# First expert layer of batches 4 to 7 computed per chosen expert instead of for all three experts

## The reference, cut to what matters

```python
h = _layernorm(x)
router_input = concatenate([h, modality_ratio], axis=-1)
gate_scores = softmax(router_input @ gate_w + gate_b)
top_val, top_idx = top_k(gate_scores, 2)
top_val = top_val / (sum(top_val) + 1e-8)
pre = einsum('bsd,edf->ebsf', h, w1) + b1
act = stack([tanh(pre[0]), gelu(pre[1]), silu(pre[2])])
expert_out = einsum('ebsf,efd->ebsd', act, w2) + b2
for i in range(2):
    moe_out += top_val[..., i:i+1] * expert_out[top_idx[:, 0, i], batch]
x = x + tanh(g_ffn[0]) * moe_out
```

## Time and profile before

| | us |
|---|---|
| median of 3 runs | 724.17 (723.84 to 725.5) |
| the profiled execution | 722.57 |
| its span | 720.8 |
| PE busy | 698.6 (97%) |
| DVE busy | 544.8 (76%) |
| ACT busy | 357.4 (50%) |
| POOL busy | 419.2 (58%) |
| mean granted TensorE clock | 0.997 |

### The profile page before, as it was taken

How to read it: one execution, slowest core, us unless ns; L and a number is a source line. 1 busy time by engine, 2 the same in 40 slices (tenths; PEclk the granted TensorE clock), 3 DMA queues, 4 the chain that set the end, 5 groups by cost and what they waited for, 6 DMA issues and landing times.

```text
span 720.8 us, 11347 instructions
## 1 busy us (share of the span) xinstructions
PE 698.6 (97%) x3478; PEld 585.7 (81%) x3478; DVE 544.8 (76%) x908; ACT 357.4 (50%) x955; POOL 419.2 (58%) x356
## 2 busy tenths in 40 slices
PE   7799998999999999999999999999999889999998
PEld 5688887888888888888888888888888667788886
DVE  6478686788788887888878788787887984478832
ACT  7424633554545545455454545545455675772130
POOL 4698764766667566665666657666676542473020
PEclk9999999999999999999999999999999999999999
DMA  8887566323222141131322213112222410230101
GB/s 292 290 245 283 207 207 200 89 59 88 60 76 73 30 119 58 58 88 61 85 59 82 64 36 110 58 58 88 69 78 59 120 59 28 74 117 1 58 1 59
DMA packets 66110, 71.09 MB, mean 99 GB/s; under 512 B 8592, under 2 KB 42384, under 8 KB 66064
## 3 DMA queue, kind: packets, MB, share of 16 engines
q1 hardware_dynamic: 65680, 69.51, 30.8%
q0 software_dynamic: 384, 1.05, 0.5%
HBM read 51.66 MB, written 18.87 MB: 98 GB/s over the span
## 4 chain that ended last, share of the span: by engine, by line
PE 89%; DVE 3%; ACT 2%; DMA 2%; POOL 2%; issue 1%; SPq 1%; ACTq 0%; POOLq 0%; DVEq 0%
PE q L272 39%; PE y L262 28%; PE o L621 5%; PE s L573 5%; PE pt L479 4%; PE s L575 2%; PE s L262 2%; PE o L262 2%; PE pt L262 2%; ACT prob L869 1%; DMA prob<-rope_rows,posi 1%; POOL rot L1044 1%; DMA rows<-ctx_t 1%; DMA wraw<-in_L_xattn_Wq 1%; DVE split L1153 1%
## 5 line engine op out<-in xcount | busy, mean ns | idle before, releaser
L272 PE MATMUL q<-xT_hi,big 128*128 128x512 f32 x704 | 237.1, 402 | 0.4 <-issue 0.4
L262 PE MATMUL y<-big,split 128*128 128x512 f32 (+1 forms) x784 | 191.6, 390 | 2.9 <-DVE split L1153 2.9
L262 PEld LDWEIGHTS y<-big,split 128*128 128x128 f32 x784 | 146.7, 188 | 34.2 <-DVE split L1153 3.9
L272 PEld LDWEIGHTS q<-xT_hi,big 128*128 128x128 f32 x704 | 132.9, 189 | 27.6 <-issue 0.6
L272 PE MATMUL q<-xT_lo,big 128*128 128x512 f32 x352 | 137.5, 391 | 0.0
L1100 POOL TENSOR_TENSOR roped<-rot 128x512 f32<-128x512 f32 x59 | 76.2, 1292 | 104.3 <-DVE rot L1177 104.3
L869 ACT ACTIVATE prob<-scores,nmax 128x128 f32<-128x128 f32 x256 | 99.9, 392 | 22.1 <-DVE nmax L1278 22.1
L857 ACT ACTIVATE big<-roped 128x512 fp32r<-128x512 f32 x64 | 40.5, 634 | 140.6 <-POOL roped L1100 136.1
L1116 POOL TENSOR_TENSOR prob<-prob,prec 128x512 f32<-128x512 f32 x64 | 66.6, 1040 | 50.4 <-DVE prec L1292 50.4
L1104 POOL TENSOR_TENSOR big<-roped,big 128x512 fp32r<-128x512 f32 x64 | 82.7, 1293 | 13.2 <-ACT big L857 13.2
L1092 POOL TENSOR_TENSOR big<-wraw,big 128x512 fp32r<-128x512 f32 x64 | 83.0, 1298 | 0.0
(11 more groups left out here) (187 smaller groups left out, 1160.2 us busy)
## 6 DMA issues: line engine op xcount, KB each, us to landing
wraw<-in_L_xattn_Wq SPq DMA_DIRECT2D x32, 256.0 KB
wraw<-in_L_xattn_Wo SPq DMA_DIRECT2D x32, 256.0 KB
kv<-k_scratch SPq DMA_DIRECT2D x64, 128.0 KB, 2.5
kv<-v_scratch SPq DMA_DIRECT2D x64, 128.0 KB, 2.8
wraw<-in_L_ffn_w SPq DMA_DIRECT2D x28, 256.0 KB
v_scratch<-split SPq DMA_DIRECT2D x12, 512.0 KB, 4.1
k_scratch<-split SPq DMA_DIRECT2D x10, 512.0 KB, 3.2
k_scratch<-kv SPq DMA_DIRECT2D x6, 512.0 KB, 3.6
```

What stands on the lines that cost most here:

```text
L262: mm = pe.matmul(bank_[:, :], stationary(s, c), moving(m, c), start=(c == 0 and n == 0), stop=(c == EC - 1 and n == 2))
L272: mm = pe.matmul(bank_[:, :].rearrange("p (b t) -> p b t", b=BH), weights[s][:, c, h * P:(h + 1) * P], source[m][:, half * BH:(half + 1) * ...
```

## The change

Batches 0 to 3 are left as they are. For batches 4 to 7 the 12 tiles of all experts are replaced by 8 tiles, one for each batch and slot ("pair" j = 0 to 7; 0 to 3 are slot 1 and 4 to 7 are slot 0 of batches 4 to 7).

- `pair_first(j)` on PE: xT of the batch is stationary, and w1 of the chosen expert moves, its block number read into a register from `pick_row`. Tokens lie on the partitions, so that b1 can't be a per-partition bias.
- `pair_add(j)` on DVE: the bank plus the b1 row of each of the two experts that the slot may hold, into two SBUF tiles. The b1 rows are loaded by three broadcast DMAs into `rows`.
- `pair_act(j)` on ACT: both functions, in place. For slot 1 they are silu and gelu, in an order that alternates with j; for slot 0 tanh and gelu.
- `pair_select(j)` on DVE: predicated copy of the second over the first.
- `pair_transpose(j)` on PE: four transposes into `tbank`; `pair_hi_(j)` on ACT and `pair_lo_(j)` on DVE split it; two buffers in `split`.
- The second layer goes by `second_tile(u)`. The four first-layer tiles that stood between tile 11 and the second layer are no more there.
- The second w1[0] goes to block 5 of `big` (where the hi and lo parts of slot 0 of batches 0 to 3 are), and its hi parts wait for second-layer tile 3 (`f2` of 4) instead of first-layer tile 15. SP waits for the last pick of batches 0 to 3 before the b1 rows and these four chunks.
- DVE: bias(0), then bias(u+1) and add_slot(u) for u = 0 to 6, then the pairs. Two small operations are added ahead of `picks_ok`.

```diff
+EXPERT_BLOCK = (0, 1, 2, 0, 4, 3, 5)
+FIRST = [(e, f) for e in range(NX) for f in range(EC)]
+PAIRS = [(slot, BH + k) for hf, slot, k in SECOND if hf == 1]
+SLOT_EXPERTS = ((0, 1), (2, 1))
...
+        b1row = [rows[:, e, :] for e in range(NX)]
+        def pair_at(j):
+            return split[:, (2, 0)[j % 2], :, :]
+        def both(j):
+            return kept[2 * (j % 2):2 * (j % 2) + 2]
+        def turn_of(j):
+            return (1, 0) if PAIRS[j][0] == 1 and j % 2 == 1 else (0, 1)
...
             for n in range(W_A + KVH * W_PER + LAG_Y, W_END):
+                if n == W_C + 6 * EC:
+                    sp.wait_ge(f_pick, EC)
+                    for e in range(NX):
+                        sp.dma_start(b1row[e], bcast(b1[e], E)).then_inc(b1_in, 16)
                 w_load(n, expert_chunk(n)).then_inc(w_in[n % NW], 16)
...
+            def second_tile(u):
+                hf, slot, k = SECOND[u]
+                j = u - B
+                if u == 0:
                     pe.wait_ge(w_lo, W_C + 6 * EC)
                     pe.wait_ge(picks_ok, 1)
+                if hf == 1:
+                    pe.wait_ge(pair_lo, j + 1)
+                elif k == 0:
+                    pe.wait_ge((keep_lo, pick_lo)[slot], EC)
+                e = pe.value_load(pick_row[0:1, slot * B + hf * BH + k:slot * B + hf * BH + k + 1],
+                                  min_val=0, max_val=NX - 1)
+                if u < 2:
+                    pe.wait_ge(y_acc, UNITS - 1 + u)
+                elif u >= 4:
+                    pe.wait_ge(f_acc, u - 3)
...
+            def pair_first(j):
+                slot, b = PAIRS[j]
+                at = 2 * B + slot * BH + b - BH
+                n = pe.value_load(pick_row[0:1, at:at + 1], min_val=0, max_val=5)
+                if j == 0:
+                    pe.wait_ge(h_lo, B)
+                if j == BH:
+                    pe.wait_ge(w_lo, W_END)
+                if j < 2:
+                    pe.wait_ge(f_act, len(FIRST) - 1 + j)
+                else:
+                    pe.wait_ge(f_z, 2 * (j - 1))
+                project(pe, qbank[j % 2], lambda a, c: xT[a][:, b, c, :],
+                        lambda a, c: big[:, bass.ds(n, 1), a, c * 512:(c + 1) * 512].rearrange(
+                            "p n k -> p (n k)")).then_inc(f1, 1)
+
+            def pair_transpose(j):
+                pe.wait_ge(f_sel, j + 1)
+                if j >= 1:
+                    pe.wait_ge(pair_lo, j)
+                transpose4(tbank, lambda c: both(j)[0][:, c * P:(c + 1) * P], f_t)
...
-            for l in range(NX * EC, (NX + 1) * EC):
-                first_layer(l)
-            second_layer(0, 0)
-            second_layer(0, 1)
-            for l in range((NX + 1) * EC, 2 * NX * EC):
-                first_layer(l)
-            second_layer(1, 0)
-            second_layer(1, 1)
+            for u in range(B - 1):
+                second_tile(u)
+            for j in range(B):
+                pair_first(j)
+                if j >= 1:
+                    pair_transpose(j - 1)
+                if j != 1:
+                    second_tile(B + j - 2 if j >= 2 else B - 1)
+            pair_transpose(B - 1)
+            second_tile(2 * B - 2)
+            second_tile(2 * B - 1)
...
                 if n == W_C + 6 * EC:
-                    act.wait_ge(f1, 4 * EC)
+                    act.wait_ge(f2, BH)
...
+            def pair_act(j):
+                for n, which in enumerate(turn_of(j)):
+                    e = SLOT_EXPERTS[PAIRS[j][0]][which]
+                    act.wait_ge(f_z, 2 * j + n + 1)
+                    act.activation(both(j)[which], both(j)[which], (ACT.Tanh, ACT.Gelu, ACT.Silu)[e]).then_inc(f_fn, 1)
+
+            def pair_hi_(j):
+                act.wait_ge(f_t, j + 1)
+                if j >= 1:
+                    act.wait_ge(f2, B + j - 1)
+                else:
+                    act.wait_ge(y_done, UNITS)
+                act.activation(pair_at(j)[:, 0, :], tbank[:, :], ACT.Copy).then_inc(pair_hi, 1)
...
             for f in range(EC):
                 w_expert_hi(n + 13 + f)
+            pair_act(0)
+            for j in range(1, B):
+                pair_hi_(j - 1)
+                pair_act(j)
+            pair_hi_(B - 1)
...
+            ts(pick_row[:, 2 * B:2 * B + BH], out_of[:, 0, BH:B], -4.0, 5.0, ALU.mult, ALU.add)
+            ts(pick_row[:, 2 * B + BH:2 * B + 2 * BH], in_it[:, 1, BH:B], -1.0, 1.0, ALU.mult, ALU.add)
...
+            def pair_add(j):
+                for n, which in enumerate(turn_of(j)):
+                    if n == 0:
+                        dve.wait_ge(f1, len(FIRST) + j + 1)
+                        if j == 0:
+                            dve.wait_ge(b1_in, 16 * NX)
+                            dve.wait_ge(keep_lo, EC)
+                        if j >= 2:
+                            dve.wait_ge(f_t, j - 1)
+                    dve.tensor_tensor(both(j)[which], qbank[j % 2][:, :], b1row[SLOT_EXPERTS[PAIRS[j][0]][which]], ALU.add
+                                      ).then_inc(f_z, 1)
+
+            def pair_select(j):
+                slot, b = PAIRS[j]
+                dve.wait_ge(f_fn, 2 * j + 2)
+                dve.copy_predicated(both(j)[0], masks[:, slot, b:b + 1].to_broadcast([P, 512]), both(j)[1]
+                                    ).then_inc(f_sel, 1)
+
+            def pair_lo_(j):
+                dve.wait_ge(pair_hi, j + 1)
+                subtract_hi(pair_at(j)[:, 1, :], tbank[:, :], pair_at(j)[:, 0, :], pair_lo)
...
-            for u in range(B):
-                bias(u)
+            bias(0)
+            for u in range(B - 1):
+                bias(u + 1)
                 add_slot(u)
...
+            for j in range(B):
+                pair_add(j)
+                if j >= 1:
+                    pair_lo_(j - 1)
+                pair_select(j)
+                if j != 1:
+                    add_slot(B + j - 2 if j >= 2 else B - 1)
+            pair_lo_(B - 1)
+            add_slot(2 * B - 2)
+            add_slot(2 * B - 1)
```

More of the change, by code:

```diff
@@ L192, in build @@
         f2, f_acc, f_bias = sem("f2"), sem("f_acc"), sem("f_bias")
-        b2_in = sem("b2_in")
+        b1_in, b2_in = sem("b1_in"), sem("b2_in")
+        f_z, f_fn, f_sel, f_t = sem("f_z"), sem("f_fn"), sem("f_sel"), sem("f_t")
+        pair_hi, pair_lo = sem("pair_hi"), sem("pair_lo")
         out_done = sem("out_done")
@@ L202, in build @@
         w1_at = [[block_of(n, s) for s in range(2)] for n in (0, 1, 0)]
-        w2_at = [[block_of(n, s) for s in range(2)] for n in (2, 3, 4)]
         w2_all = big[:, 2:2 + NX, :, :]
@@ L369, in expert_target @@
         def expert_target(n):
-            (layer, e), k = expert_matrix(n)
-            return (w1_at, w2_at)[layer][e], k
+            at = EXPERT_BLOCK[(n - W_C) // EC]
+            return [block_of(at, s) for s in range(2)], (n - W_C) % EC
         block = stack.enter_context(nc.Block())
@@ L666, in first_layer @@
                     pe.wait_ge(f_act, l - 1)
-                project_tile(pe, qbank[l % 2], w1_at[e], f, xT, hf).then_inc(f1, 1)
+                project_tile(pe, qbank[l % 2], w1_at[e], f, xT, 0).then_inc(f1, 1)
             groups(pe, unit)
             second_bank = [ybank[0], ybank[1], pbank, obank]
-            def second_layer(hf, n):
-                if hf == 0 and n == 0:
+            def second_tile(u):
+                hf, slot, k = SECOND[u]
+                j = u - B
+                if u == 0:
@@ new lines, in second_tile, with stationary @@
+                e = pe.value_load(pick_row[0:1, slot * B + hf * BH + k:slot * B + hf * BH + k + 1],
[4 more added lines that the diff above has]
+                    pe.wait_ge(f_acc, u - 3)
+                def stationary(a, c):
+                    if hf == 1:
+                        return pair_at(j)[:, a, c * P:(c + 1) * P]
+                    return picked[slot][a][:, c, k * P:(k + 1) * P]
@@ new lines, in second_tile @@
+                project(pe, second_bank[u % 4], stationary,
+                        lambda a, c: w2_all[:, bass.ds(e, 1), a, c * 512:(c + 1) * 512].rearrange(
+                            "p e n -> p (e n)")).then_inc(f2, 1)
+            def pair_first(j):
[13 more added lines that the diff above has]
+                            "p n k -> p (n k)")).then_inc(f1, 1)
@@ L935, in first_act @@
                     act.wait_ge(route_mm, 1)
[L936 to L942, removed]
+                if e == 2 and f >= 2:
+                    act.wait_ge(pick_lo, f - 1)
+                to = (kept[f], rows[:, f, :], rot[:, f % 2, :])[e]
@@ L943, in first_act, with keep_hi_ @@
                 act.activation(to, qbank[l % 2][:, :], (ACT.Tanh, ACT.Gelu, ACT.Silu)[e], bias=b1c[:, e, f:f + 1]
                                ).then_inc(f_act, 1)
-            def keep_hi_(k):
-                hf, f = k // EC, k % EC
-                if k == 0:
+            def keep_hi_(f):
+                if f == 0:
                     act.wait_ge(s_done, UNITS)
```

(33 more changed lines are left out.)

38 lines of the change are left out of this document (6 added, 32 removed).

## The result

| | before | after |
|---|---|---|
| median of 4 runs, us | 724.38 (723.84 to 725.5) | 731.32 (729.94 to 734.1) |
| the profiled execution | 722.57 | 730.14 |
| its span | 720.8 | 728.4 |
| PE busy | 698.6 | 696.9 |
| mean granted clock | 0.997 | 0.990 |

The ratio is 1.0100 with an interval of 1.0077 to 1.0123: slower by 6.9 us, where the prediction had +6.3 and 730.5.

A forecast was written before the change was run, and what follows sets the result against it. PE bounded the kernel before (97% busy); after, DVE's queue sets the first transposes at 679.9. Adding 41.6 + 1.5 + 0.4 + 0.4 ends PE at 723.8, last addition 724.65 against 718.35: +6.3, 730.5 us, range 727.0 to 733.8.

The forecast's parts named there:

- PE gains 7.4 us: PE's tail: 12 tiles go, 8 come (-10.9 us), eight times four transposes come (+3.5); 68.8 us of work, 7.4 less.
- First wait, about 5.3 us and the read, costing nothing by itself: Ahead of second-layer tile 0: PE waits for POOL's last w2[1] lo part, then reads the register; hidden within the second wait.
- DVE reaches pair_add(0) at 675.6: DVE's queue, behind bias(7) and add_slot(6): 25.0 us of work from 650.01, later POOL subtractions moving the start to 675.6 us.
- The collision with POOL: Bias instructions on DVE slowed beside POOL's w1[0] subtractions: 2.6 us lost instead of 2.0, bounds 0 and 4.
- Chain of pair 0, 4.2 us: From pair_add(0) to first transposes: addition, silu, table load, gelu, predicated copy, hand-overs; 4.2 us, transposes start at 679.9.
- Second wait 4 to 5.7 us: Ahead of the first transposes: PE is done at 674.2, or up to 1.7 later, and waits 4 to 5.7 us.
- Pair 1's wait 1.5 and the clock +0.4: Behind the first transposes: PE waits 1.5 us for pair 1's copy; half clock adds net 0.4, bounds 0 and 3.4.
- Starting anew, 0.4 us, and the rest: PE restarting from an empty queue: some 0.2 us each, twice, 0.4 us; bounds 0 and 8.
- PE sets the end: Rival: pair_add(0) starts by 669.9, so PE, not DVE, sets the end; 722.5 us (5%) or 723.7 (4%).
- the drain: Rival: table loads cost a drain more, chains of pairs 0 and 1 longer by 1.4 us each; 733.3 us, 5%.
- DVE and POOL miss each other: Rival: DVE's bias instructions and POOL's subtractions do not meet; 2.6 us less, 728 us, 9%.
- The clock costs more: Rival: uncovered half-clock stretches follow both long waits and pair 1's wait; +1.5 to +3.4 us, 733 us, 14%.

The follow-up runs named there:

- e3: Changed kernel plus 24 filler matmuls into an unused bank between first-layer tile 11 and second-layer tile 0; 732.31 us, ratio 1.0097.
- e1: Kernel before, with only first-layer tiles 12 to 15 moved behind second-layer tiles 0 to 7 on PE; 734.24 us, ratio 1.0142.
- e5: Changed kernel with ACT's four hi copies of the second w1[0], and POOL's four subtractions with them, moved behind pairs 1 and 2; 728.37 us, ratio 1.0055.
- e2: Changed kernel with bias(5) to bias(7) moved from ahead of pair_add(0) to between the pairs; 727.93 us, ratio 1.0040.
- e4: Changed kernel with silu for all functions of the pairs, so no table loads there (other output values); 728.24 us, ratio 1.0042.
- e7: Changed kernel plus 12 filler matmuls of 512 columns between pair_first(1) and the first transposes; 730.36 us, ratio 1.0100.
- e6: Changed kernel reordered per engine: pair_first(0) and (1) right behind tile 11, pair_add(0) and (1) ahead of bias(0), bias(3) to (7) between pairs; 721.50 us, ratio 0.9966.
- e8: Kernel of e6 with bias(0) ahead of pair_add(0) on DVE; 719.83 us, ratio 0.9929.
- e9: Kernel of e6 measured again on a different chip, with more rounds; 720.23 us, ratio 0.9928.

## Why the prediction was right

It had the sign, the size (+6.3 for +6.9 in the medians, +7.2 in the tails) and the mechanism: DVE's queue sets the first transposes. They were forecast 33.3 us behind POOL's end and started 33.29 behind it. That it is so exact is luck, as the steps show:

- **PE gains 7.4 us.** Right as work: from 691.81 the period of a pair is 5.92 us, where it had 5.88, and four transposes take 0.44.
- **First wait, about 5.3 us and the read, costing nothing by itself.** It was 6.2. The start behind POOL's end took 1.02 us (646.98 to 648.00), where I had 0.4. That it costs nothing was shown by e3 (down to 0.8, the first transposes at the same place); that it would cost 8.3 us with PE as the bound, by e1.
- **DVE reaches pair_add(0) at 675.6.** It was 676.17; 0.4 of the difference was already there ahead of the tail. The collision with POOL took 3.3 us instead of 2.6: a term mis-sized by 0.7, since all four subtractions met bias instructions. Against it, the rest of DVE's work took 22.5 us, and not the 23.0 that are left of the stretch before without its 2.70 us of idle and its collision. e5 shows the term, e2 the step as a whole.
- **Chain of pair 0, 4.2 us.** 676.17 to 680.23 is 4.06. (675.6 + 4.2 is 679.8, where the forecast has 679.9.) e4 shows the table load in it.
- **Second wait 4 to 5.7 us.** It was 2.6, outside these bounds and outside the 4 to 6 us that I named as what the profile would show: PE came to it at 677.6 instead of 674.2, by the slower start and by a half-clock stretch that cost PE 2.4 us (pair_first(1) ended 29.6 us behind the start of tile 0 instead of 27.2), where the bound was 1.7. It changed nothing in the sum, as the transposes did not wait for PE.
- **Pair 1's wait 1.5 and the clock +0.4.** The wait was 0.2 because half clock filled the rest: pair 1's copy ended at 685.25, forecast 684.55, and of the 0.7 between them 0.4 was there at the first transposes. e7's rows put the clock's net share at 0.4, as the term has it, and its tail at no more than 0.8.
- **Starting anew, 0.4 us, and the rest.** This is the term that was most mis-sized. From 685.30 to PE's end at 725.12 are 39.8 us; 13 tiles and 7 times four transposes are 38.4. The 1.4 us more are mostly at the starts: tile 8 takes 0.12 and 3.01 us, tile 14, behind the last transposes, 0.22 and 3.03 instead of 2.72. 0.12 + 0.29 and 0.22 + 0.31 are 0.9 of it. This term is about what the tail is longer by than the sum.

Of the rivals, "PE sets the end" fell by e2 and e3, the drain by ACT's rows and "DVE and POOL miss each other" by DVE's rows. "The clock costs more" priced this at +1.5 to +3.4 us, which the changed kernel doesn't pay: the first half-clock stretch cost nothing (e3) and the second 0.4 to 0.8 us (e7).

## What to carry to other kernels

Before work is taken out of an order written by hand, ask what its time covers: here 10.9 us of tiles covered a wait for a weight split that alone (e1) costs more than the change saves. Then add up the queue of the engine on which the new chain begins, because work that was free beside PE (24 bias instructions) becomes the critical path as soon as the first new instruction stands behind it. The saving is there once the new chain starts early and the old work goes between its links (e6, e8, e9: 0.3 to 0.7% below the kernel before).

## What the runs showed of the hardware beyond what I expected

- A second-layer tile with a register-selected operand started 1.0 us behind the semaphore that released it (646.98 to 648.00; 1.01 in e1 too), not 0.4, although the read itself is usually 0.30; this one took 0.49. With matmuls on PE up to shortly before it, it was 1.0 in e3 and 0.8 in e6, of which PE stood idle for 0.8 and 0.6.
- Half clock behind the 6.2 us wait cost PE 2.1 us on two tiles in e1 (7.49 instead of 5.44), more than I had allowed. A wait of 1.8 us ahead of the transposes in e9 was followed by half clock and a tail 1.7 us longer than in e6, where a wait of 1.2 us in the same place was not. Behind 1.3 us (e4) and 1.1 us (e2) the clock did not fall either.
- Three broadcasts of a 2 KB row to 128 partitions (256 KB each), followed by four weight loads of 256 KB, kept the chain of e6 for 6.3 us; the median of the three from issue to landing was 4.0 us, and a kv load of 128 KB lands in 2.5.
